# Two routed expert layers on one core: down weights split where they are used, weight loads issued earlier

## The reference

```python
# first FFN: ein is 8 x 640 x 256, W1 is 256 x 1024, W2 is 1024 x 256 for each expert
h = jax.nn.relu(jnp.einsum('ecd,edf->ecf', ein, W1))
eout = jnp.einsum('ecf,efd->ecd', h, W2).reshape(E * cap, D)
# second FFN: W11 and W12 are 256 x 512, W2 is 512 x 256 for each of the 8 experts
gate = jnp.einsum('bsh,ehi->bsei', x, W11)
value = jnp.einsum('bsh,ehi->bsei', x, W12)
fused = gate * jax.nn.sigmoid(gate) * value
expert_out = jnp.einsum('bsei,eih->bseh', fused, W2)
gathered = jnp.take_along_axis(expert_out, topk_idx[..., None], axis=2)
out = jnp.sum(topk_scores[..., None] * gathered, axis=2)
```

## Time and profile before

| | us |
|---|---|
| median of 3 runs | 1263.85 (1263.3 to 1270.29) |
| the profiled execution's own time | 1267.65 |
| its span | 1265.9 |
| capacity stage, first transpose to last matmul | 245.0 to 502.3 |
| tile stage, first transpose to last addition issued | 878.3 to 1259.4 |
| PE busy, share of the span | 1090.2 (86%) |

### The profile page before, as it was taken

How to read it: one execution, slowest core, us unless ns; L and a number is a source line. 1 busy time by engine, 2 the same in 40 slices (tenths; PEclk the granted TensorE clock), 3 DMA queues, 4 the chain that set the end, 5 groups by cost and what they waited for, 6 DMA issues and landing times. The chain is left out here.

```text
span 1265.9 us, 27756 instructions
## 1 busy us (share of the span) xinstructions
PE 1090.2 (86%) x7956; PEld 1014.6 (80%) x7956; DVE 814.4 (64%) x2410; ACT 647.5 (51%) x2529; POOL 548.2 (43%) x605
## 2 busy tenths in 40 slices
PE   6899897299999998787999999940999999999995
PEld 5588776299999988666988888840999999999995
DVE  6699998343444433667999999961555655655563
ACT  2578786344444443056889888940333433433331
POOL 0256665343333332006668777662123322323333
PEclk9899999599999999897999999975999999999998
DMA  8700000367777763401112211125575777478843
GB/s 287 293 2 26 25 21 31 120 238 244 259 249 267 258 246 146 123 5 38 39 43 68 67 64 63 52 77 206 149 248 138 221 208 224 92 215 291 249 62 39
DMA packets 86862, 180.21 MB, mean 142 GB/s; under 512 B 8066, under 2 KB 62212, under 8 KB 82692
## 3 DMA queue, kind: packets, MB, share of 16 engines
q1 hardware_dynamic: 69412, 152.18, 34.5%
q0 software_dynamic: 17376, 27.15, 10.3%
HBM read 182.01 MB, written 69.64 MB: 199 GB/s over the span
## 5 line engine op out<-in xcount | busy, mean ns | idle before, releaser
L1278 PE MATMUL psum<-E_xT_hi,E_up_w 128*128 128x256 f32 x1248 | 231.2, 284 | 21.5 <-DMA E_up_w<-up 20.1
L1384 POOL DMA_INDIRECT out<-E_y,E_dest x78 | 121.5, 1558 | 274.4 <-DMA out<-E_y,E_dest 130.2
L607 ACT ACTIVATE L_prob<-psum,L_neg_max 128x64 f32<-128x64 f32 x768 | 229.1, 352 | 16.2 <-DVE L_neg_max L734 15.5
L1278 PEld LDWEIGHTS psum<-E_xT_hi,E_up_w 128*128 128x128 f32 x1248 | 198.5, 194 | 23.6 <-issue 22.0
L607 ACT ACTIVATION_READ_ACCUMULATOR L_prob<-psum,L_neg_max 128x1 f32 x768 | 186.6, 245 | 0.0
L1307 ACT ACTIVATE E_sg<-psum 128x256 f32<-128x256 f32 x156 | 60.0, 385 | 232.3 <-PE psum L1278 231.2
L1278 PE MATMUL psum<-E_xT_lo,E_up_w 128*128 128x256 f32 x624 | 176.9, 284 | 0.0
L1355 DVE TENSOR_TENSOR E_hf<-psum,E_sg 128x256 f32<-128x256 f32 x156 | 66.2, 425 | 122.1 <-ACT E_sg L1307 120.6
L561 PE MATMUL psum<-L_n_hi,L_pT_hi 128*128 128x256 f32 (+1 forms) x384 | 111.7, 291 | 18.3 <-DVE L_pT_lo L750 9.9
L1278 PEld LDWEIGHTS psum<-E_xT_lo,E_up_w 128*128 128x128 f32 x624 | 121.0, 194 | 0.0
L1263 PE MATMUL psum<-E_down_w,E_h_hi 128*128 128x256 f32 x624 | 117.3, 283 | 0.0
(11 more groups left out here) (206 smaller groups left out, 3139.2 us busy)
## 6 DMA issues: line engine op xcount, KB each, us to landing
E_up_w<-up SPq DMA_DIRECT2D x39, 2048.0 KB
E_down_w<-down SPq DMA_DIRECT2D x39, 1024.0 KB
w<-in_w SPq DMA_DIRECT2D x16, 1024.0 KB, 15.2
E_raw<-in_w SPq DMA_DIRECT2D x24, 512.0 KB, 5.0
E_xin<-rows SPq DMA_DIRECT2D x39, 260.0 KB, 3.0
up<-E_raw_hi SPq DMA_DIRECT2D x16, 512.0 KB, 3.3
up<-E_raw_lo SPq DMA_DIRECT2D x16, 512.0 KB, 3.3
rows<-zero SPq DMA_DIRECT2D x8, 640.0 KB
```

Of the source, the lines that this page charges most:

```text
L607: last = e.activation(prob[:, q, h * KEYS:(h + 1) * KEYS], scores_ps(k)[:, h * KEYS:(h + 1) * KEYS], ACT.Exp, bias=nmx[:, q, h, :], accum_ ...
L1278: mm = q.matmul(bank, up_w[:, par, half, w, c, m * P:(m + 1) * P], x[:, c, :], start=(k == 0), stop=(k == 3 * KC - 1))
L1384: q.indirect_dma_start(p.out[:, :], bass.IndirectOffsetOnAxis(ap=dest[:, par, c, :], axis=0), y[:, par, c, :], None, compute_op=ALU.add).t ...
```

## The change

The second layer's down weights are no longer split ahead. The capacity stage splits and stores only the two up matrices of each expert (16 splits in place of 24), the first at the fourth group of the first half of `hidden`, the second behind the next expert's weight splits. The `down1` tensor is gone. The tile stage loads the down weights as they are (512 KB) and splits them for every tile: ACT the hi part behind its first silu, POOL the lo part ahead of the indirect DMAs.

SP's order is new in both stages. In the capacity stage the tokens of the next expert come first, and w1 and w2 are loaded for the expert after the next as soon as their one buffer is free. In the tile stage the up weights of tile i+1 come first, then its rows, then its down weights.

```diff
-        def load(q, e):
-            if not is_int(e) or e > 0:
-                wait(q, s_w1lo, e)
-                q.dma_start(w1[:, :, :], w1_d[:, e, :, :]).then_inc(s_w1, 16)
-                wait(q, s_w2lo, e)
-                q.dma_start(w2[:, :, :], w2_d[:, e, :, :]).then_inc(s_w2, 16)
+        def load_w1(q, e):
+            q.wait_ge(s_w1lo, e)
+            q.dma_start(w1[:, :, :], w1_d[:, e, :, :]).then_inc(s_w1, 16)
+
+        def load_w2(q, e):
+            q.wait_ge(s_w2lo, e)
+            q.dma_start(w2[:, :, :], w2_d[:, e, :, :]).then_inc(s_w2, 16)
+
+        def load_x(q, e):
             wait(q, s_xT, TC * e)
             q.dma_start(xin[:, :, :], rows[:, e, :, :]).then_inc(s_x, 16)
...
-        def store_raw(q, k):
-            q.wait_ge(s_rhi, k + 1)
-            q.dma_start(part(0, k // 3, k % 3), raw_hi[:, :].bitcast(F32)).then_inc(s_sthi, 16)
-            q.wait_ge(s_rlo, k + 1)
-            q.dma_start(part(1, k // 3, k % 3), raw_lo[:, :].bitcast(F32)).then_inc(s_stlo, 16)
+        def load_raw(q, e, j):
+            wait(q, s_rlo, 2 * e + j - 1)
+            q.dma_start(raw[:, j, :].rearrange("p (c f) -> p c f", c=KC),
+                        ins[("w11", "w12")[j]][e, :, :].rearrange("(c p) f -> p c f", p=P)).then_inc(s_raw[j], 16)
+
+        def store_raw(q, e, j):
+            q.wait_ge(s_rhi, 2 * e + j + 1)
+            q.dma_start(p.up1[e, :, j, 0, :], raw_hi[:, :].bitcast(F32)).then_inc(s_sthi, 16)
+            q.wait_ge(s_rlo, 2 * e + j + 1)
+            q.dma_start(p.up1[e, :, j, 1, :], raw_lo[:, :].bitcast(F32)).then_inc(s_stlo, 16)
...
-                load(q, 0)
-                for k in range(2):
-                    load_raw(q, k)
+                load_x(q, 0)
+                load_w1(q, 1)
+                load_w2(q, 1)
+                for j in range(2):
+                    load_raw(q, 0, j)
                 for e in range(E):
                     if e + 1 < E:
-                        load(q, e + 1)
-                    for k in range(3 * e, 3 * e + 3):
-                        store_raw(q, k)
-                        if k + 2 < 3 * E:
-                            load_raw(q, k + 2)
+                        load_x(q, e + 1)
+                    store_raw(q, e, 0)
+                    if e + 2 < E:
+                        load_w1(q, e + 2)
+                    if e + 1 < E:
+                        load_raw(q, e + 1, 0)
+                    store_raw(q, e, 1)
+                    if e + 2 < E:
+                        load_w2(q, e + 2)
+                    if e + 1 < E:
+                        load_raw(q, e + 1, 1)
                     for h, (c0, cn) in enumerate(HALVES):
                         q.wait_ge(s_y, TC * e + c0 + cn)
                         q.dma_start(rows[:, e, c0:c0 + cn, :], y[:, h, 0:cn, :]).then_inc(s_st[h], 16)
                 for h in range(2):
                     q.wait_ge(s_st[h], 16 * E)
-                q.wait_ge(s_sthi, 16 * 3 * E)
-                q.wait_ge(s_stlo, 16 * 3 * E)
+                q.wait_ge(s_sthi, 16 * 2 * E)
+                q.wait_ge(s_stlo, 16 * 2 * E)
...
                         q.activation(h_hi[:, h, m, 0:cn * P], ps[:, UP_BANK + m % 4, 0:cn * P], ACT.Relu).then_inc(s_hhi, 1)
-                        if m == 3:
-                            split_raw(e, par, h)
-
-                def split_raw(e, par, j):
-
-                    k = 3 * e + j
-                    q.wait_ge(s_raw[(par + j) % 2], 16 * ((k + 2) // 2 if is_int(k) else (k + 2) >> 1))
-                    wait(q, s_rlo, k)
-                    wait(q, s_sthi, 16 * k)
-                    q.activation(raw_hi[:, :], raw[:, (par + j) % 2, :], ACT.Copy).then_inc(s_rhi, 1)
+                        if h == 0 and m == 3:
+                            split_raw(e, 0)
+
...
                 def body(e, par, last=False):
-                    hidden(e, par, 0)
-                    hidden(e, par, 1)
+                    hidden(e, 0)
+                    hidden(e, 1)
                     if not last:
                         split_w1(e + 1, 1 - par)
                         split_w2(e + 1, 1 - par)
-                    split_raw(e, par, 2)
+                    split_raw(e, 1)
                     if not last:
                         split_x(e + 1)
                 pairs(q, lambda e, par: body(e, par, is_int(e) and e == E - 1))
...
                 def body(e, par):
-                    split_raw(e, par, 0)
-                    split_raw(e, par, 1)
+                    split_raw(e, 0)
                     if not is_int(e) or e < E - 1:
                         split_w(e + 1, 1 - par)
-                    split_raw(e, par, 2)
+                    split_raw(e, 1)
                 pairs(q, body)
...
-                def load_down(i, par):
+                def load_w2(i, par):
                     e = expert(i)
                     new = None if is_int(i) and i < 2 else changed(i)
-                    wait(q, s_dn, TC * (i - 1))
+                    wait(q, s_w2lo, i - 1)
                     land(q, i)
-                    q.dma_start(down_w[:, par, :, :, :].rearrange("p w m d -> p (w m d)").bitcast(F32),
-                                down_d[e, :, :], cond=new).then_inc(s_w2[par], 16)
+                    q.dma_start(w2[:, par, :, :], w2_d[:, e, :, :], cond=new).then_inc(s_w2[par], 16)
...
                 load_x(0, 0)
                 load_up(0, 0)
+                load_w2(0, 0)
 
                 def body(i, par, last):
                     if not last:
+                        load_up(i + 1, 1 - par)
                         load_x(i + 1, 1 - par)
-                        load_up(i + 1, 1 - par)
-                    load_down(i, par)
+                        load_w2(i + 1, 1 - par)
                 tiles_loop(q, body)
...
                 def down(i, par):
-                    q.wait_ge(s_w2[par], 16 * nth(i))
+                    wait(q, s_w2lo, i + 1)
...
+                def split_w2(i, par):
+                    q.wait_ge(s_w2[par], 16 * nth(i))
+                    wait(q, s_dn, TC * (i - 1))
+                    q.activation(w2_hi[:, par, :, :], w2[:, par, :, :], ACT.Copy).then_inc(s_w2hi, 1)
...
                         q.activation(sg[:, m, :], ps[:, UP_BANK + m, 0:T1], ACT.Silu).then_inc(s_sg, 1)
+                        if m == 0:
+                            split_w2(i, par)
...
                 def body(i, par, last):
+                    q.wait_ge(s_w2hi, i + 1)
+                    q.tensor_tensor(w2_lo[:, par, :, :], w2[:, par, :, :], w2_hi[:, par, :, :].bitcast(F32),
+                                    ALU.subtract).then_inc(s_w2lo, 1)
                     if not is_int(i) or i > 0:
                         add(i - 1, 1 - par)
```

More of the change, by code:

```diff
@@ L1046, in split_x, with hidden @@
                                      ACT.Copy).then_inc(s_xThi, 1)
-                def hidden(e, par, h):
+                def hidden(e, h):
                     cn = HALVES[h][1]
@@ L1054, in hidden, with split_raw @@
                         q.activation(h_hi[:, h, m, 0:cn * P], ps[:, UP_BANK + m % 4, 0:cn * P], ACT.Relu).then_inc(s_hhi, 1)
-                        if m == 3:
-                            split_raw(e, par, h)
-                def split_raw(e, par, j):
-                    k = 3 * e + j
-                    q.wait_ge(s_raw[(par + j) % 2], 16 * ((k + 2) // 2 if is_int(k) else (k + 2) >> 1))
-                    wait(q, s_rlo, k)
-                    wait(q, s_sthi, 16 * k)
-                    q.activation(raw_hi[:, :], raw[:, (par + j) % 2, :], ACT.Copy).then_inc(s_rhi, 1)
+                        if h == 0 and m == 3:
+                            split_raw(e, 0)
+                def split_raw(e, j):
+                    q.wait_ge(s_raw[j], 16 * (e + 1))
+                    wait(q, s_rlo, 2 * e + j)
+                    wait(q, s_sthi, 16 * (2 * e + j))
+                    q.activation(raw_hi[:, :], raw[:, j, :], ACT.Copy).then_inc(s_rhi, 1)
                 split_w1(0, 0)
@@ L1131, in split_w, with split_raw @@
                                     ALU.subtract).then_inc(s_w2lo, 1)
[L1133 to L1137, removed]
+                def split_raw(e, j):
+                    wait(q, s_rhi, 2 * e + j + 1)
+                    wait(q, s_stlo, 16 * (2 * e + j))
+                    q.tensor_tensor(raw_lo[:, :], raw[:, j, :], raw_hi[:, :].bitcast(F32),
                                     ALU.subtract).then_inc(s_rlo, 1)
@@ L1163, in experts_top2 @@
         up_w = p.sb(st, n + "up_w", [P, 2, 2, 2, KC, F1], F32R)
-        down_w = p.sb(st, n + "down_w", [P, 2, 2, FC, D], F32R)
+        w2 = p.sb(st, n + "w2", [P, 2, FC, D])
+        w2_hi, w2_lo = (p.sb(st, n + x, [P, 2, FC, D], F32R) for x in ("w2_hi", "w2_lo"))
         xin = p.sb(st, n + "xin", [P, 2, TC, DW])
@@ L1174, in experts_top2 @@
         s_w, s_w2, s_x = ([S(f"{x}_loaded{j}") for j in range(2)] for x in ("w1", "w2", "x"))
-        s_xT, s_xThi, s_xTlo = S("xT"), S("xT_hi"), S("xT_lo")
```

(8 more changed lines are left out.)

## The result

The changed kernel takes 1277.62 us, the median of four runs (1276.33 to 1278.87), against 1263.85 before. The ratio on record is 1.0091, with a 95% interval of 1.0062 to 1.0119; the two medians alone give 1.0109. The forecast was 1256 with a range of 1238 to 1273; the time lies above it. The profiled execution has a span of 1277.1.

What follows compares the result with a forecast made beforehand. PE, busy 86% of the span, was taken as the bound, its idle and throttled time recoverable. Terms -15.8 + 7.7 - 26.7 + 19.6 + 2.1 + 2.0 + 2.0 + 1.0 = -8.1, from 1263.85 to 1256; range 1238 to 1273.

Steps and rivals of the forecast that it cites:

- The new splits, +1: Tile stage: ACT's and POOL's per-tile splits mostly fit free time; DVE operations held by POOL's split cost 1 us in all.
- rival (b): Tile stage: PE and POOL bind each other, DVE-POOL loop 0.4 us longer per tile, 1270, at worst 1291; chance 0.17.
- Capacity stage, steady, -15.8: Capacity stage: moving the second raw split removes all six PE stalls on DVE's PSUM copy, saving 15.8 us.
- Capacity stage, start, +7.7: Capacity stage start: first raw loads stand behind w2; PE stops 5.7 us, slow matmuls add 2.0.
- Tile stage, up load, -26.7: Tile stage: up weights no longer wait behind the row load, so their stalls and throttling go, saving 26.7 us.
- the 2.0 that I left: Tile stage: 2.0 us of the 26.7 kept, as some tiles run 0.2 slow without a wait.
- Tile stage, its start, +2: Start of tile stage: PE waits about 2 us for w2, second up load and rows of tile 1.
- Rows late, +19.6 +2.1: Tile stage: rows queue behind up loads, 14 waits of 1.2 to 1.6 us, 19.6, plus 2.1 for slower matmuls.
- rival (a): Tile stage: the queue does not hold up rows, so 19.6 us do not come back, 1236; chance 0.10.
- Rival (c), the clock: Tile stage: each of 14 transpose stalls lowers the granted clock, +27, 1283; chance 0.08.
- signs of being wrong: Row waits above 2 with clock 0.5 behind, load-free tiles of 9 us or more, or rows landing 3 us after issue.
- Rival (d): Capacity stage: stalls stay because another wait of ACT or DVE takes their place, 1271; chance 0.12.

Runs made afterwards that it cites:

- experiment 1: Changed kernel with the tile stage's lo split of the down weights on DVE instead of POOL: 1249.84 us, ratio 0.9872.
- Experiment 6: Changed kernel with the down weights' lo split on DVE, raw matrices first at the start, metadata earlier, rows ahead of up weights: 1225.79 us, ratio 0.9708.
- experiment 10: Experiment 6 with the lo split of the down weights back on POOL: 1274.54 us, ratio 1.0116.
- Experiment 5: Changed kernel with the two raw matrices loaded ahead of the second w1 and w2 at the capacity stage's start: 1265.67 us, ratio 1.0027.
- experiment 7: Kernel before with two metadata steps, not one, behind each hf on DVE in the tile stage: 1241.63 us, ratio 0.9829.
- experiment 4: Kernel before with the up load issued ahead of the load of rows in the tile stage: 1254.43 us, ratio 0.9911.
- 9: Experiment 6 with the up load again issued ahead of the rows: 1238.33 us, ratio 0.9834.

## Why the prediction was wrong, step by step

**The new splits, +1: this step failed.** The mechanism was the one named in rival (b), the loop of DVE and POOL through `E_xT_lo` and `E_y`. Its size was wrong. I took the held operation to be the metadata step just ahead of `E_xT_lo`, which leaves about 1.8 us from the end of the split to the first `E_y`. The rows show 2.98 (1218.75 to 1221.73) and, in the other tile, 2.3: the split comes earlier, the operation that it holds is `E_wt` or `E_h_lo`, and three to five more stand behind that ahead of `E_xT_lo`. POOL's part, the split of 2.41 and the pair, was right: 2.41 + 2.98 + 1.29 to the first DMA + 3.41 for the pair is 10.1, and the row's 2.97 has the split begin before the second DMA's 1.55 end. The loop is 9.4 to 10.1 where I had 8.7, and PE's tile is 8.63.

There is a slip in the sum as well: its terms, 2.41 + 0.7 + 1.5 + 0.8 + 3.4, make 8.8 and not 8.7. Even 8.7 is 0.07 over a tile, 2.5 us in 36 tiles, and 8.8 would be 6, where I charged 1.

Between experiment 1 and the changed kernel the tile stages differ by 391.8 - 367.0 = 24.8; between 6 and 10, where no late rows lie under it, by 50. The rule of the Trainium skill that I cited (SBUF — State Buffer, two separate sides) is borne out by the trace: a DVE operation with two SBUF inputs, 0.41 alone, took up to 3.94 and ended right behind the split. I had priced its worst case from one tile's slack, 1.0 each, and given it a third of 0.17; measured are 1.15 a tile, and 1.35 in experiment 10. A loop that is "already at the tile's length" by a sum that leaves out the queue behind the held operation deserved more.

**Capacity stage, steady, -15.8:** right. Six experts went from 193.0 to 177.3, -15.7 where these six were to give 14.8; PE never waits for `E_y`, an expert takes 29.6. Experiment 5, without the cost at the start, has the whole stage 16.9 below the 257.3 of before.

**Capacity stage, start, +7.7:** right. PE stopped for 5.2 (5.7 forecast), and the half behind it took 8.3 at a granted clock of 0.69, in place of 5.9; experiment 5 gives 7.9.
```profile
260.60:268.90 8.30, 8.28 (x50) 8.30 (x51) 4.09 (x10) 3.11 (x9) 1.35 (x1) 0.69 0.32 127
```

**Tile stage, up load, -26.7:** right; its cause, the metadata ahead of the load, is shown by experiment 7, which takes away the late issue alone and gets 19.8 of it. Experiment 6, where neither load is late, is 24.2 below before, against 26.7 less the 2.0 that I left.

**Tile stage, its start, +2:** did not come. PE waits for up weights once, 5.4, and not again for the second load; from the stage's first transpose to up(1) it is 16.7 us before and after.

**Rows late, +19.6 +2.1:** the mechanism is right (4, 9), so rival (a) fell, but the size is too large: 8.6 to 9.9 us in 10 to 12 waits with the split on DVE, 13.2 in seven in experiment 4, since often one tile of a pair waits little. In the tile stage, 9 against 6, it is 11.4, about half of the 21.7. In the changed kernel most of it hides under the longer tiles: 4.9 is seen.

**Rival (c), the clock:** no such fall behind the stops of up to 1.2 in experiment 1. In the changed kernel one stop of five, the longest with 2.51, did bring it:
```profile
923.90:928.90 5.00, 5.00 (x30) 5.00 (x31) 2.83 (x10) 1.21 (x3) 0.63 (x1) 0.66 0.19 37
```
That is one of the signs of being wrong that I named, a wait on rows above 2 with the lower clock behind it, but it came once and not 14 times. The other sign, tiles without a load of 9 us or more, is the one that tells.

**Rival (d)** did not happen.

**The sum.** With +24.8 for +1.0 the forecast becomes -8.1 + 23.8 = +15.7, too high by the late rows and the start. By stage, I had -8.1 for the capacity stage and 0 for the tile stage. By stage the change did -9.0 + 17.7 = +8.7; the medians differ by 13.8. The rest lies in the stages that it did not touch (+2.4 between the two profiled executions) and in how far each of these lies above its median (3.8 and 1.3).

**What stays open.** Why the second attention takes 364.6 in one execution and 371.7 in another. Where a hold begins, since it reaches back ahead of the split's row. And why DVE gets in at one seam between two pieces on POOL and not at the others, and whether it would at all of them if they stood further apart: not tried.

## What to carry to other kernels

Work put on an idle engine can hold a busy one: look first whether the two share something, and which operations of the busy engine are touched. When two engines wait on each other in a ring, sum the whole ring, with everything that is queued behind the held instruction, and compare it with the period; a sum within a few per cent of the period gives no cover. Cutting the work on the other engine into pieces did not help here; taking operations out of the way behind the held one did. Before reordering transfers, ask what the late one waits for: six small steps moved earlier on DVE beat the new order.

## What the runs showed of the hardware that was not expected

The same subtraction of 128x1024 took 1.22 us on DVE and 2.41 on POOL; the "idle" engine was the dearer place by itself. Four POOL instructions back to back held a DVE operation for 3.11, as one of 2.97 did, in 10 tiles; in 27 others DVE got in once among them and was held again. And stops of PE of much the same length had different sequels in experiment 4: behind 3.19 the granted clock was 0.66, behind 2.93 (ahead of the transposes of tile 28) the next 3.5 us ran at 1.00.
